# Mixture-of-experts stage of a fused layer: 24 steps of up to 512 rows with W2 stationary, in place of 40 steps of 256 rows

## The reference, cut to what matters

```python
cap = int(math.ceil(CF * N / E))          # 1229 rows for each of 8 experts
probs = jax.nn.softmax(x @ Wr + br, axis=-1)
gates, ids = jax.lax.top_k(probs, K)      # K = 2
...                                       # each expert keeps its cap best (token, choice) pairs
xg = x[disp_tok].reshape(E, cap, Dm)      # Dm = 128
h = jax.nn.silu(jnp.einsum('ecd,edh->ech', xg, W1) + b1[:, None, :])   # hidden 512
out = jnp.einsum('ech,ehd->ecd', h, W2) + b2[:, None, :]
gated = out * disp_g.reshape(E, cap, 1)
y = jnp.zeros((N, Dm), x.dtype).at[disp_tok].add(gated.reshape(E * cap, Dm))
```

## Time and profile before

| | |
|---|---|
| runs, median | 954.77 us |
| the profiled execution | 954.1 us, span 952.4 us |
| mean granted TensorE clock | 0.835 of 2.4 GHz |
| PE busy in the whole span | 702.2 us (74%) |
| DVE, ACT, POOL busy | 640.4, 484.3 and 464.0 us |
| experts stage | about 651 to 902.7 us |
| combine stage | about 902.7 to 952.4 us |

### The profile page before, as it was taken

The page is one execution under the profiler, slowest core; times in us unless marked ns, Lnnn a source line. Parts: engine busy times, 40 slices in busy tenths (PEclk is TensorE's granted clock), DMA queues, the critical chain, the costliest instruction groups (busy, mean ns, idle before and its releaser), DMA issues. The chain is left out here.

```text
span 952.4 us, 15550 instructions
## 1 busy us (share of the span) xinstructions
PE 702.2 (74%) x4187; PEld 559.7 (59%) x4187; DVE 640.4 (67%) x2281; ACT 484.3 (51%) x1243; POOL 464.0 (49%) x590
## 2 busy tenths in 40 slices
PE   7457999999999993999898334275677867787600
PEld 3225777777777762989898224243566756676500
DVE  7656999999999954799898576793223222322387
ACT  4754566676666654878685224162222222222356
POOL 7502666676666762243333500004666666666462
PEclk8876999999999995999999555556978889888955
DMA  8920000000000006000000075003122212221197
GB/s 216 365 88 1 1 1 1 2 1 1 2 1 1 1 2 177 1 2 2 2 0 2 0 113 67 0 0 79 45 67 65 68 44 66 64 69 42 45 304 216
DMA packets 73233, 52.96 MB, mean 56 GB/s; under 512 B 11744, under 2 KB 67048, under 8 KB 72896
## 3 DMA queue, kind: packets, MB, share of 16 engines
q1 hardware_dynamic: 67312, 41.61, 16.5%
q0 software_dynamic: 5120, 10.37, 4.2%
q10 hardware_dynamic: 720, 0.05, 0.1%
HBM read 28.04 MB, written 24.18 MB: 55 GB/s over the span
## 5 line engine op out<-in xcount | busy, mean ns | idle before, releaser
L817 DVE SCALAR_TENSOR_TENSOR s_cv<-s_pU,tap_w,s_cv 128x256 f32<-128x256 f32 x384 | 159.6, 477 | 20.0 <-ACT s_cv L761 19.6
L1834 ACT ACTIVATE e_h<-e_pH,e_b 128x256 f32<-128x256 f32 x160 | 65.3, 472 | 166.7 <-remote 105.7
L1776 POOL DMA_INDIRECT e_xg<-token_rows,token_of x80 | 82.0, 1025 | 127.6 <-issue 127.6
L1810 PE MATMUL e_pH<-e_xgT,e_w 128*128 128x256 f32 x320 | 93.3, 443 | 51.2 <-issue 50.5
L1783 POOL DMA_INDIRECT choice_rows<-e_yo,choice_of x80 | 80.5, 1006 | 63.0 <-DVE e_yo L1879 39.6
L1810 PEld LDWEIGHTS e_pH<-e_xgT,e_w 128*128 128x128 f32 x320 | 67.3, 221 | 65.5 <-issue 54.8
L1820 PE MATMUL e_pO<-e_w,e_h 128*128 128x128 f32 x640 | 87.1, 287 | 6.1 <-issue 5.4
L1820 PEld LDWEIGHTS e_pO<-e_w,e_h 128*128 128x128 f32 x640 | 81.7, 204 | 8.9 <-issue 8.9
L637 POOL TENSOR_TENSOR s_xa<-s_xt,arena 128x512 f32<-128x512 f32 x32 | 34.4, 1075 | 103.2 <-ACT s_xt L779 103.2
L1872 DVE TENSOR_TENSOR e_ysum<-e_pO,e_b 128x256 f32<-128x256 f32 x40 | 17.0, 425 | 95.3 <-PE e_pO L1820 44.7
L666 PE MATMUL s_pU<-arena,w_in 128*128 128x262 f32 x256 | 72.3, 407 | 11.7 <-DVE s_cv L817 8.4
(11 more groups left out here) (285 smaller groups left out, 1862.8 us busy)
## 6 DMA issues: line engine op xcount, KB each, us to landing
choice_rows<-zrow SPq DMA_DIRECT2D x16, 512.0 KB, 7.2
arena<-choice_rows SPq DMA_DIRECT2D x32, 256.0 KB, 5.1
token_rows<-arena SPq DMA_DIRECT2D x8, 520.0 KB, 12.6
n_x<-in_L_attn_x_dram SPq DMA_DIRECT2D x8, 512.0 KB, 7.6
arena<-in_L_attn_x_dram SPq DMA_DIRECT2D x8, 512.0 KB, 4.6
e_w<-in_L_ffn_W_dram SPq DMA_DIRECT2D x16, 256.0 KB
out_dram<-arena SPq DMA_DIRECT2D x16, 256.0 KB, 4.4
decay_rows<-arena SPq DMA_DIRECT2D x2, 1024.0 KB, 4.7
```

Of the source, the lines that this page charges most:

```text
L817: v.scalar_tensor_tensor(out=by_tile(cv[:, p % 2, m, :]), in0=columns(m)[:, :, tap:tap + P], scalar=tap_w[:, m, tap:tap + 1], in1=by_tile( ...
L1776: g.indirect_dma_start(xg[:, n % RING, i, :], None, table, bass.IndirectOffsetOnAxis(ap=token_of[:, G * n + i:G * n + i + 1], axis=0), bou ...
L1810: ins = pe.matmul(pH[n % 2][half_][:, ROWS * c:ROWS * (c + 1)], we1[:, expert(n), P * f:P * (f + 1)], xgT[:, n % 2, :], start=True, stop=True)
L1834: ins = a.activation(hb[:, n % 2, f, :], pH[n % 2][half_][:, ROWS * c:ROWS * (c + 1)], ACT.Silu, bias=be1[:, expert(n), f:f + 1])
```

## The change

A step is now two, three or four blocks: the first expert's steps have 2, 4, 4, the last one's 4, 4, 2, the others' 4, 3, 3. There are 24 steps, three for each expert, and still 80 blocks. `up` is four products of up to 512 columns into four single banks. `down` now holds a quarter of `W2` stationary and moves `h` of the whole step: four products, whose result has features in the partitions. So ACT adds `b2` as a bias column (`outs`) into `oT`, a new PE stage `back` transposes each block again into `pB`, and DVE multiplies by the gates in one operation for the step. All biases are loaded once, as 40 rows, and turned to columns by one transpose. PE's round is up(i-2), down(i-3), back(i-4), turn(i); ACT's is silus(i-2), outs(i-3); DVE's is results(i-4), fetched(i), gates(i); POOL's is fetch(i), leave(i-5). `xg` and `yo` lie in two arenas that are free at that time and so are called `arena` in the rows.

```diff
-            G = ROWS // P
-            TOTAL = EXPERTS * ESTEPS
-            RING = 2 * ESTEPS
-            LAG = 6
+            sizes = []
+            for e in range(EXPERTS):
+                sizes += (2, 4, 4) if e == 0 else (4, 4, 2) if e == EXPERTS - 1 else (4, 3, 3)
+            TOTAL = len(sizes)
+            STEP = TOTAL // EXPERTS
...
+            RING = 8
+            LAG = 5
...
-            pH = [[pst(f"e_pH{k}{h}") for h in range(2)] for k in range(2)]
-            pO = [pst("e_pO0"), pst("e_pO1")]
+            pH = [pst(f"e_pH{c}") for c in range(NF)]
+            pO, pB = pst("e_pO"), pst("e_pB")
...
+                sp.dma_start(brows[0:EXPERTS * NF, :], b1.rearrange("e (c p) -> (e c) p", p=P)).then_inc(s_rows, 16)
+                sp.dma_start(brows[EXPERTS * NF:NR, :], b2).then_inc(s_rows, 16)
                 for e in range(EXPERTS):
-                    par = e % 2
                     if e >= 2:
-                        sp.wait_ge(s_po, ESTEPS * (e - 1))
-                        sp.wait_ge(s_ys, ESTEPS * (e - 1))
...
-                    sp.dma_start(be1[:, par, :], b1[e].rearrange("(c p) -> p c", p=P)).then_inc(s_we[par], 16)
-                    sp.dma_start(be2[:, par, :], b2[e].partition_broadcast(P)).then_inc(s_we[par], 16)
+                        need(sp, s_po, STEP * (e - 1) - 1)
+                    sp.dma_start(we1[:, e % 2, :], W1[e]).then_inc(s_we[e % 2], 16)
+                    sp.dma_start(we2[:, e % 2], W2[e].rearrange("(c p) d -> p c d", p=P)).then_inc(s_we[e % 2], 16)
...
                 def up(n):
                     weights(pe, n)
                     need(pe, s_xgT, n)
...
+                    w = P * sizes[n]
+                    for c in range(NF):
+                        need(pe, s_h, NF * n + c, NF)
+                        pe.matmul(pH[c][:, 0:w], we1[:, expert(n) % 2, P * c:P * (c + 1)], xgT[:, n % 3, 0:w],
+                                  start=True, stop=True).then_inc(s_ph, 1)
                 def down(n):
-                    need(pe, s_h0, n)
-                    need(pe, s_h1, n)
-                    need(pe, s_ys, n, 2)
-                    for i in range(G):
-                        for c in range(NF):
-                            ins = pe.matmul(pO[n % 2][:, P * i:P * (i + 1)], hb[:, n % 2, c, P * i:P * (i + 1)],
-                                            we2[:, expert(n), c, :], start=(c == 0), stop=(c == NF - 1))
+                    need(pe, s_h, NF * n + NF - 1)
+                    need(pe, s_o, n, 1)
+                    w = P * sizes[n]
+                    for c in range(NF):
+                        ins = pe.matmul(pO[:, 0:w], we2[:, expert(n) % 2, c, :], hb[:, n % 2, c, 0:w],
+                                        start=(c == 0), stop=(c == NF - 1))
                     ins.then_inc(s_po, 1)
-                staged([(1, up), (0, turn), (2, down)])
+                def back(n):
+                    need(pe, s_o, n)
+                    need(pe, s_yo, n, 1)
+                    for i in range(sizes[n]):
+                        ins = pe.transpose(pB[:, P * i:P * (i + 1)], oT[:, n % 2, P * i:P * (i + 1)], ident[:, :])
+                    ins.then_inc(s_pb, 1)
+                pe.wait_ge(s_rows, 32)
+                pe.transpose(pB[:, 0:NR], brows[:, :], ident[0:NR, 0:NR]).then_inc(s_turned, 1)
+                pe.wait_ge(s_bias, 1)
+                staged([(2, up), (3, down), (4, back), (0, turn)])
...
-                staged([(0, silus)])
+                def outs(n):
+                    need(a, s_po, n)
+                    need(a, s_pb, n, 2)
...
+                    a.activation(oT[:, n % 2, 0:w], pO[:, 0:w], ACT.Identity, bias=bcols[:, f:f + 1]).then_inc(s_o, 1)
...
+                staged([(2, silus), (3, outs)])
...
                 def fetched(n):
                     need(v, s_pt, n)
-                    need(v, s_ph1, n, 2)
+                    need(v, s_ph, NF * n + NF - 1, 3 * NF)
...
                 def results(n):
...
+                    need(v, s_pb, n)
...
+                    v.tensor_tensor(yo[:, k, 0:w, :], pB[:, 0:P * w].rearrange("p (i d) -> p i d", d=D),
+                                    gate[:, k, 0:w].unsqueeze(2).broadcast_to([P, w, D]), ALU.mult).then_inc(s_yo, 1)
-                staged([(0, fetched), (0, gates_of), (2, results)])
+                staged([(4, results), (0, fetched), (0, gates_of)])
```

More of the change, by code:

```diff
@@ L1672, in build @@
             st.callback(stage_over)
-            G = ROWS // P
-            TOTAL = EXPERTS * ESTEPS
-            RING = 2 * ESTEPS
-            LAG = 6
+            sizes = []
[3 more added lines that the diff above has]
+            STEP = TOTAL // EXPERTS
+            starts = [sum(sizes[:n]) for n in range(TOTAL + 1)]
+            assert starts[TOTAL] == COLS
+            WIDE = 4
+            RING = 8
+            LAG = 5
+            NR = EXPERTS * NF + EXPERTS
             def sbt(name, shape, dt=F32):
@@ L1781, in leave @@
                     need(g, s_yo, n)
-                    for i in range(G):
-                        g.indirect_dma_start(choice, bass.IndirectOffsetOnAxis(ap=choice_of[:, G * n + i:G * n + i + 1], axis=0),
+                    for i in range(sizes[n]):
+                        c = starts[n] + i
+                        g.indirect_dma_start(choice, bass.IndirectOffsetOnAxis(ap=choice_of[:, c:c + 1], axis=0),
                                              yo[:, n % RING, i, :], None, bounds_check=2 * TOKENS - 1,
@@ L1805, in up @@
                     need(pe, s_xgT, n)
[L1806 to L1812, removed]
@@ L1827, in silus @@
                 def silus(n):
-                    weights(a, n)
                     need(a, s_po, n, 2)
[L1830 to L1834, removed]
-                                               bias=be1[:, expert(n), f:f + 1])
-                        ins.then_inc(done, 1)
-                staged([(0, silus)])
+                    w = P * sizes[n]
+                    for c in range(NF):
+                        f = NF * expert(n) + c
+                        need(a, s_ph, NF * n + c)
+                        a.activation(hb[:, n % 2, c, 0:w], pH[c][:, 0:w], ACT.Silu, bias=bcols[:, f:f + 1]).then_inc(s_h, 1)
+                def outs(n):
+                    need(a, s_po, n)
+                    need(a, s_pb, n, 2)
+                    w = P * sizes[n]
+                    f = EXPERTS * NF + expert(n)
+                    a.activation(oT[:, n % 2, 0:w], pO[:, 0:w], ACT.Identity, bias=bcols[:, f:f + 1]).then_inc(s_o, 1)
+                a.wait_ge(s_turned, 1)
+                a.activation(bcols[:, :], pB[:, 0:NR], ACT.Copy).then_inc(s_bias, 1)
+                a.wait_ge(s_bias, 1)
+                staged([(2, silus), (3, outs)])
                 def rooted(g):
```

63 lines of the change are left out of this document (28 added, 35 removed).

## The result

The changed kernel takes 941.13 us (median of 4 runs, 940.72 to 944.51) against 954.77 (median of three runs; a fourth, of 3254.91 us, is left out). The ratio, of the means of these runs, is **0.9864, interval 0.9836 to 0.9893**: 13 us faster, where 29 were forecast. On another chip the same two kernels stood at 0.9929 (0.9905 to 0.9952), 7 us apart. The traced execution took 944.5 us with a span of 942.8, 9.6 us less than before.

The account below looks back on a forecast made before the run. POOL's DMA list bounds the kernel, with 38.5 us of waiting for `yo` to win. 954.1 - 38.5 + 4 + 4 + 2 = 925.6, plus 0.7 from profiled execution to median: 926 us; range 917 to 950.

Parts of the forecast that it names:

- What bounds the kernel: Stage is as long as POOL's DMA list: 211.0 us own pace plus 38.5 us waiting for `yo`, TensorE's word held back.
- Middle: POOL's waits for `yo` between start and end: between 0 and 10 us, taken as 4, with fewer records a block.
- 2.0 to 2.8 matmul records per us: Rate at which TensorE's word gets through while POOL issues; need falls from 4.9 to 2.6, about even.
- End: After the last gather, 20 scatters; the last two need `yo`(23) after 23.8 us, TensorE needs 22; 2 us of waiting taken.
- Start: First scatter stands behind 20 gathers, ending 678.3; its `yo` comes at 681.2, a 2.9 us wait, taken as 4.
- the hold: Word that TensorE is done is held back while POOL issues without a pause; a stop costs 3.4 us every 18.96 us.
- The hold does not ease: Rival: word goes by semaphore or columns; some 13 stops of about 3 us stay, less 5 at the end; 949, chance 0.16.
- Lead too short: Rival: POOL's lead falls from 21.1 to 17.6 us, stops of 6.7 us; 996, or 975 with half of them; chance 0.10.
- sign for the hold: In the profile: stops of 3 us or more every 15 to 20 us, DVE and ACT starting together after POOL's last DMA.
- The clock: Rival: TensorE's clock falls in idle times; 1016 at 1.2 GHz throughout; sign, eight `up` records take 7 us; chance 0.03.
- POOL issues faster: Rival: POOL gains up to 23 us as DVE's 80 L1879 operations go; 903, chance 0.03.
- The port rule: A VectorE operation can lock GpSimd out of a shared port; up to 23 us off POOL's list, forecast took 0.

Follow-up runs that it names:

- e9: Changed kernel with one POOL write of unread zeros (0.8 us added) ahead of every step's scatters, 24 breaks; ratio 0.9846 to the kernel before.
- e5: Changed kernel with work left out: `up` and `down` compute only half of a step's columns; ratio 0.9869 to the kernel before, 941.6 us.
- e3: Changed kernel with each `up` and `down` product cut in two halves of its columns, twice the records; ratio 1.0051 to the kernel before, 959.6 us.
- e17: e3 with e16's breaks, one write of zeros ahead of the scatters of steps 0 to 18; ratio 0.9960 to the kernel before.
- e6: Changed kernel with `up`, `down` and `back` one round nearer to the turn (1, 2, 3 rounds behind); ratio 1.0005 to the kernel before, 954.5 us.
- e7: Changed kernel with the newest rows turned first in TensorE's round instead of last; ratio 1.0055 to the kernel before.
- e16: e9 with its breaks only ahead of the scatters of steps 0 to 18; ratio 0.9819 to the kernel before, 937.1 us.
- e18: e16 with four more breaks, ahead of the gathers of steps 1 to 4; ratio 0.9841 to the kernel before, 940.4 us.
- e2: Changed kernel with POOL writing a step back 8 steps after its gathers instead of 5, ring of 12; ratio 0.9931 to the kernel before.
- e1: The changed kernel run again with no edit; ratio 0.9929 to the kernel before, 948.8 us.

## Why the prediction was half right

- **What bounds the kernel**: right. POOL's pace stayed (161.0 us busy for 162.5, 0.30 between DMAs), and e9 with e5 shows that the middle stops are held word.
- **Middle, 4 us forecast, 15.2 measured: this step failed.** The prediction had word get through at "2.0 to 2.8 matmul records per us" while POOL issues, and a need that falls from 4.9 to 2.6. The sum compared that need with a rate that the runs do not bear out. In the held state the word of an `up` product takes most often some 2.1 us, with two records of 384 columns, four of 192 (e3) or two of 192 (e5); in the kernel before, the words of a pair of products (four records of 256) come 1.4 to 3.5 us apart, 2.16 twice. The prediction's rate came from two stretches of one kernel, so its unit was a guess, as it said. What is there instead is two states: a free one, in which word is on time, and a held one, in which it falls behind in either kernel. Fewer records lengthen the free time (e3, e17), and the number of stops nearly halved, eleven to six. The records explain a part of that: with twice of them (e3) there are eight. The order of the parts counts too (e6, e7), and how the rest divides is not shown.
- **End, 2 us forecast, 9.7 measured.** I had TensorE start the last rounds on time. It was held until 859.8; freed of that (e16) the end waits 2.9.
- **Start, 4 us forecast, 6.5 measured.** The working had a chain of 29.3 us from the first gather to the first scatter with all word on time. It was 32.8, because the word of the first `down` was held for 6.3 us. Had it come at once, the next `down` could have followed the `up` that ended at 676.02, and by e18's 1.5 us from the end of that `down` to the scatter the first scatter would have come at about 681.1 (an estimate), 3.4 us of waiting. So the chain was about right, and the hold, taken as nothing here, is some 3 us.
- The sum: the waits were 2.5 + 11.2 + 7.7 = 21.4 us above the forecast, so that 7.1 of the 28.5 were left; POOL's shorter DMAs gave 1.5, an earlier first gather 0.5 and a shorter combine 0.6: 9.7, and the span has 9.6.
- **The rivals.** "The hold does not ease" (949) was nearest in kind, with stops that recur, but wrong in saying that only the end would gain. "Lead too short" was wrong (e2); the stops are 3 to 4 us, not 6. The prediction's sign for the hold, stops of 3 us or more each 15 to 20 us, came with stops 13 to 38 us apart. The clock: eight `up` records of 512 columns took 3.60 us at 767, not 7; and the middle's clock is 0.83 to 0.97 between 700 and 850. "POOL issues faster": the 80 operations went and a DMA still takes 1.00 us. The port rule of the Trainium skill, page "SBUF — State Buffer", section "Who interferes with whom", would have given up to 23 us here; POOL's DMAs became 1.5 us shorter in all.

The clock by stretch, the counterpart of the earlier trace rows:

```profile
700.00:750.00 50.00, 38.33 (x114) 19.96 (x113) 6.89 (x24) 14.47 (x24) 34.46 (x35) 0.90 0.20 55
750.00:800.00 50.00, 40.80 (x117) 20.77 (x116) 8.63 (x30) 16.75 (x29) 33.26 (x34) 0.83 0.24 64
800.00:850.00 50.00, 38.06 (x126) 20.80 (x125) 7.28 (x25) 13.38 (x23) 35.88 (x36) 0.97 0.26 69
```

Open: what in the chip holds the word, and what exactly brings the hold on. A break takes away POOL's issuing and, for a moment, the DMAs' traffic; no run parts the two. That the free time is shorter with twice the records hints at a count, but e18 was held from 725 to 790 with e16's breaks and records in the middle, and e16 was not.

## What to carry over

Where an engine waits for another that the profile shows as done long before, look at whose word is late and what the other engines were doing; a rate read in one kernel has no sure unit until another kind of work gives the same one. Where GpSimd issues indirect DMAs back to back beside TensorE, 1.1 us without a DMA every seven DMAs or so paid for itself (ratio to the kernel before 0.9819 and 0.9846 with; 0.9864, 0.9929 and, with breaks too small to matter, 0.9924 without). Fewer, larger products helped, more lead did not.

## What was not expected of the hardware

TensorE's semaphore events come up to 14.6 us after their products in the changed kernel (17.3 in e5) while GpSimd issues indirect DMAs every 1.31 us, those of ACT and DVE 0.01 us after their instructions. The lateness has two states. In the free one all is on time for 13 to 22 us of the same DMAs after a stop (11 to 15 in e1, 5 to 9 in e3); in the held one the words of a step's four `up` products come mostly at multiples of about 0.7 us (0.7, 1.4, 2.1, 2.8). It ended 1.3 to 2.6 us after the last DMA where the traces were read for it.
